# An LSTM and a GRU in one loop: the GRU's candidate and new state move one tick behind its gates

## The chip, the core and the metric

The kernel runs on one core of one Trainium2 chip. The metric is the device time of one execution in microseconds (us). TensorE does the matmuls, VectorE (DVE) and ScalarE (ACT) the element-wise work, GpSimd (POOL) a few sums, SyncE (SP) issues most of the DMA transfers. Each engine takes its own instructions in the order in which they are written; semaphores order the engines among each other.

## The reference: what is computed

`x` is 32 x 128 x 512 (batch, time, features), `cond_1024` is 32 x 512. First an LSTM runs over the 128 steps, with the condition as its first state, and its output is added to `x`. Then a GRU runs over the result, with a product of the condition in each gate, and its output is added as well.

```
# LSTM step, h0 = cond, c0 = 0
a = x_t @ Wx + b + h @ Wh                   # 32 x 2048
i, f, o = sigmoid(first three quarters of a); g = tanh(last quarter)
c = f * c + i * g ;  h = o * tanh(c)
y = x + hs                                   # input of the GRU
# GRU step, g0 = 0, vz = cond @ C_z + b_z, vr and vh likewise
z = sigmoid(y_t @ W_z + g @ U_z + vz)
r = sigmoid(y_t @ W_r + g @ U_r + vr)
hh = tanh(y_t @ W + (r * g) @ U + vh)
g = (1 - z) * g + z * hh
out = y + gs
```

Both recurrences are serial. The GRU's step s needs the LSTM's step s, and inside a step of the GRU the candidate `hh` needs the gate `r`: two products in a row (`U_z, U_r`, then `U`) with element-wise work between them.

## The kernel before

A tick is one turn of the main loop. In tick t the kernel works on step t of the LSTM and on step s = t - 1 of the GRU (`LAG = 1`), so there are 129 ticks. Each engine has a function `tick(t, n, i)` with its share of the tick, and the order of its instructions is the order of the code. Nothing else sets the order: there is no scheduler.

A step has five products on TensorE, each of 48 matmuls with float16 halves (a state and a weight are split in a high and a low part, and three of the four products of the parts are taken):

- `ps_l<-wh,h2T`: the LSTM's state times Wh, 512 columns per matmul;
- `ps_g<-w,y2T`: the GRU's input times W_z, W_r and W, 384 columns;
- `ps_g<-u,g2T`: the GRU's state times U_z and U_r, 256 columns;
- `ps_l<-wx,x2T`: x of the next step times Wx, 512 columns; it depends on no recurrence;
- `ps_g<-u,rg2T`: r * g times U, 128 columns.

Before the change TensorE does them in just this order in each tick. Between them the other engines work: `gates` (sum with the bias, VectorE L541), sigmoid and tanh (ScalarE), `ig_fc`, `tg_cell` (the cell, L696 and L698), `tanh_c`, `h_nat`, its transpose `hT` (L670), its high part (ScalarE L462) and low part (VectorE L538). For the GRU: the sum of the gates `zr` (L541), its sigmoid (ScalarE L457), `rg`, `rgT`, `rg2T` high and low; then the sum of `cand`, its tanh (L479), `zc`, `g_nat`, `gT` (L763), and `g2T` high (ScalarE L485) and low. GpSimd adds `yT = xT + hT` and the output, and scales y. Four steps make a group. One tick in four turns the next group's x and works out its scales (`turn`, `lstm_scales`), one stores a finished group (`turn_out`), one makes the low part of x, one takes its largest value.

The head of the kernel is different. Weights arrive as float32, and their split needs a scale from the sum of their squares. So the first ticks carry the preparation besides the steps: ScalarE squares each weight (`wh_squared`, `w_squared`, `u_squared`, L343) and writes the high halves (`wh_high`, `w_high`, `u_high`, L346); TensorE sums the squares over the partitions (L826); VectorE works out the scales (`weight_scale`) and writes the low halves (`wh_low`, `w_low`, `u_low`, L538, half a weight slab each). As long as a weight isn't split, its products run on the float32 weights (L789, until the LSTM's step 4 and the GRU's step 8). Wh must be split before tick 4, W and U before the GRU's step 8. The preparation is spread over the ticks by hooks: `after_state`, `after_keep` and `after_cand` on VectorE, `after_state` and `after_cand` on ScalarE. In tick 1 TensorE also does the condition's three products (`ps_c<-u,h0T` and `ps_c<-o_area,h0T`), which wait for the weights C_z, C_r and C to arrive.

Of the kernel before, what the change touches and what calls it, by code (L numbers as in the profile page):

```python
# [5 lines left out]
def lstm_then_gru(nc, x, cond, wx, wh, b0, w_z, u_z, c_z, b_z, w_r, u_r, c_r, b_r, w_h, u_h, c_h, b_h, out):  # L6
# [4 lines left out]
    ALU = mybir.AluOpType  # L11
# [9 lines left out]
    LAG = 1  # L21
    FL, F = 4, 8
# [27 lines left out]
    with ExitStack() as ctx:  # L50
# [230 lines left out]
        def _(pool):  # L281
# [50 lines left out]
            add_out(T - 1, (T - 1) % U, NG - 1)  # L332

        @block.scalar
        def _(act):
# [106 lines left out]

            def tick(t, n, i):
                s, q, r = t - LAG, n % Q, n // Q
                group = 2 * i + r
                if runs_lstm(t):
                    act.wait_ge(tg_sum, t + 1)
                    nc.scalar.activation(tg_cell[:, 0:P], gates[:, 3 * P:4 * P], ACT.Tanh)  # L448
                    act.wait_ge(ifo_sum, t + 1)
                    nc.scalar.activation(ifo, ifo, ACT.Sigmoid).then_inc(ifo_done, 1)  # L450
                    act.wait_ge(cell_done, t + 2)
                    nc.scalar.activation(tanh_c[:], cell, ACT.Tanh).then_inc(tanh_c_done, 1)
                if t == T_WH:
                    after_state(t)
                if runs_gru(t):
                    act.wait_ge(zr_sum, s + 1)
                    nc.scalar.activation(zr[:], zr[:], ACT.Sigmoid).then_inc(zr_done, 1)  # L457
# [11 lines left out]
                if (q == 1 and 0 < group < NG - 1) or t == 2:  # L469
                    act.wait_ge(xT_done, group + 2)  # L470
                    act.wait_ge(scl_done, group + 2)
                    if t >= 2 * Q:
                        act.wait_ge(gates_ps, t - 1)
                    nc.scalar.mul(x2T[:, 1 - r, HI, :], xT[:, 1 - r, :], a_x(1 - r)).then_inc(x_hi, 1)
                if t != T_WH:
                    after_state(t)
                if runs_gru(t):
                    act.wait_ge(cand_sum, s + 1)
                    nc.scalar.activation(cand[:], cand[:], ACT.Tanh).then_inc(cand_done, 1)  # L479
                    if F - 1 <= s < T - 1:  # L480
                        m_next = (n - LAG + 1) % U
                        act.wait_ge(gT_done, s + 1)
                        if m_next % Q == 0:
                            act.wait_ge(scg_done, (s + 1) // Q + 1)
                        nc.scalar.mul(g2T[:, HI, :], gT[:, s % 2, :], a_g(m_next // Q)).then_inc(g_hi, 1)  # L485
# [5 lines left out]
        def _(dve):  # L491
# [112 lines left out]
            def after_state(t):  # L604
# [5 lines left out]
                if t == T_WH:  # L610
# [5 lines left out]

                    dve.wait_ge(bias1_in, 16 * GG * J)
                    dve.wait_ge(cond_ps, 1)
                    link(nc.vector.tensor_tensor(term1[:], ps_c[:, 0:GG * P], term1[:], ALU.add))

            def after_keep(t):
                if t == T_WH + 1:
                    wh_low(1, 0)
                if t == T_WH + 2:
                    wh_low(2, 1)
                if t == T_WU_SCALE:
                    weight_scale(2, 2 * K, GG, "a_w", w1_scale)
                if t == T_WU_SCALE + 1:
                    w_low(0, 0)
                if t == T_WU_SCALE + 2:  # L630
                    w_low(1, 1)
                if t == T_WU_SCALE + 3:
                    u_low(0, 0)
                if t == T_WU_SCALE + 4:
                    u_low(1, 1)

            def after_cand(t):
                if t == T_WH:

                    wh_low(0, 0)  # L640
                    wh_low(0, 1)
# [35 lines left out]
            def tick(t, n, i):  # L677
                s, q, r = t - LAG, n % Q, n // Q
                group = 2 * i + r
                m = (n - LAG) % U  # L680
                r_s = m // Q
                r_h = (n + 1) % U // Q
                r_n = (m + 1) % U // Q
                lstm, gru = runs_lstm(t), runs_gru(t)
                if lstm:
                    if q == 0:
# [4 lines left out]
                           ).then_inc(ifo_sum, 1)  # L691
                after_sums(t)
# [6 lines left out]
                if t == T_WH:  # L699

                    new_state(t, n)
                    after_state(t)
                if gru:
                    if m % Q == 0:
                        dve.wait_ge(scg_done, (group if m // Q == r else group - 1) + 1)
                    dve.wait_ge(zr_ps, s + 1)
                    undone(zr[:], ps_g[s % 2][:, 0:2 * P], r_g(r_s), term1[:, 0:2 * P]).then_inc(zr_sum, 1)
                if lstm and t != T_WH:
                    new_state(t, n)
                if gru:  # L710
                    dve.wait_ge(zr_done, s + 1)
# [261 lines left out]
```

## Time and profile before

| | us |
|---|---|
| median of 3 runs | 1243.46 |
| lowest and highest | 1242.91, 1243.78 |
| the profiled execution | 1244.18 |
| its span, first to last instruction | 1242.4 |
| TensorE busy | 1205.5 (97% of the span) |
| VectorE busy | 872.4 (70%) |
| ScalarE busy | 445.0 (36%) |
| GpSimd busy | 278.0 (22%) |

The table gives busy times of one profiled execution over its span. The time runs 1.8 us longer than the span of the same execution. Shares are averages over a head (the first 150 us, with the loading and the splitting of the weights), some 1,070 us of equal ticks, and a tail of some 20 us in which the LSTM has ended; in the head VectorE and ScalarE have more to do than in the rest.

### The profile page before, as it was taken

What the parts mean: (1) busy time and instruction counts of PE and PEld (TensorE: products, weight loads), DVE (VectorE), ACT (ScalarE), POOL (GpSimd) and SP (SyncE); (2) the same over time, 40 slices, a digit from 0 to 9 for tenths busy, and PEclk for the clock granted to TensorE, in tenths of its full rate; (3) what the DMA queues carried; (4) which work ended last, traced back from release to release, by engine and by line L of the source; (5) the groups of instructions that cost most, each with busy time, mean ns of one, the idle gap of its engine ahead of it and who ended that gap; (6) DMA issues with size and microseconds to landing.
All of it is one profiled execution on the core that took longest, in us unless ns stands there. A gap on an engine that the chain in (4) does not pass through costs nothing.

```text
span 1242.4 us, 67987 instructions
## 1 busy us (share of the span) xinstructions
PE 1205.5 (97%) x31013; PEld 763.8 (61%) x31013; DVE 872.4 (70%) x2681; ACT 445.0 (36%) x1078; POOL 278.0 (22%) x520
## 2 busy tenths in 40 slices
PE   5889999999999999999999999999999999999996
PEld 1457666666666666666666666666666666666664
DVE  2568877777777777777776777777777777677765
ACT  5555233333333333333333333333333333333332
POOL 3100222222212222222222221222222222222221
PEclk9899999999999999999999999999999999999998
DMA  9900100111110111110011111011111001110001
GB/s 304 317 9 12 20 10 14 21 20 20 21 19 6 20 21 21 20 21 12 12 21 21 20 21 20 5 19 20 21 21 21 13 11 21 20 20 12 12 8 24
DMA packets 142000, 39.50 MB, mean 32 GB/s; under 512 B 135760, under 2 KB 136016, under 8 KB 140688
## 3 DMA queue, kind: packets, MB, share of 16 engines
q1 hardware_dynamic: 140016, 34.49, 12.9%
q8 instruction: 243, 3.98, 1.3%
q0 software_dynamic: 640, 0.53, 0.2%
q14 instruction: 45, 0.37, 0.1%
q10 hardware_dynamic: 1056, 0.13, 0.1%
HBM read 26.74 MB, written 8.39 MB: 28 GB/s over the span
## 4 chain that ended last, share of the span: by engine, by line
PE 93%; SPq 3%; DVE 2%; DMA 1%; issue 1%; ACT 0%; POOLq 0%; POOL 0%; DVEq 0%
PE ps_l L780 51%; PE ps_g L780 38%; PE ps_g L789 3%; SPq L239 2%; DMA o_area<-in_L_cond_C_dram 1%; PE ps_l L789 1%; SPq L243 1%; PE ps_bound L822 0%; DVE wh L538 0%; DVE u L538 0%; DVE zr L541 0%; SPq L248 0%; SPq L250 0%; PE ps_c L789 0%; ACT zr L457 0%
## 5 line engine op out<-in xcount | busy, mean ns | idle before, releaser
L780 PE MATMUL ps_l<-wh,h2T 128*32 128x512 f16 x5952 | 344.4, 380 | 3.3 <-DVE wh L538 3.3
L780 PE MATMUL ps_l<-wx,x2T 128*32 128x512 f16 x5952 | 342.8, 379 | 0.0
L780 PE MATMUL ps_g<-w,y2T 128*32 128x384 f16 x5760 | 256.2, 327 | 0.0
L780 PEld LDWEIGHTS ps_l<-wx,x2T 128*32 128x32 f16 x5952 | 160.6, 97 | 134.2
L780 PEld LDWEIGHTS ps_l<-wh,h2T 128*32 128x32 f16 x5952 | 154.6, 97 | 138.7 <-DVE wh L538 3.6
L780 PEld LDWEIGHTS ps_g<-w,y2T 128*32 128x32 f16 x5760 | 155.3, 97 | 92.3
L320 POOL TENSOR_TENSOR yT<-xT,hT 128x128 f32<-128x128 f32 x128 | 61.9, 484 | 589.8 <-DVE hT L670 589.8
L780 PE MATMUL ps_g<-u,g2T 128*32 128x256 f16 x5760 | 178.5, 273 | 0.8 <-ACT g2T L485 0.8
L780 PEld LDWEIGHTS ps_g<-u,g2T 128*32 128x32 f16 x5760 | 154.7, 97 | 16.9 <-issue 1.2
L541 DVE SCALAR_TENSOR_TENSOR zr<-ps_g,sc,term 128x256 f32<-128x256 f32 x128 | 61.9, 484 | 108.0 <-PE ps_g L780 100.5
L304 POOL TENSOR_TENSOR o_area<-yT,gT 128x128 f32<-128x128 f32 x128 | 58.6, 458 | 307.3 <-DVE gT L763 307.3
L541 DVE SCALAR_TENSOR_TENSOR gates<-ps_l,sc,term 128x128 f32<-128x128 f32 (+1 forms) x256 | 111.4, 476 | 13.7 <-PE ps_l L789 6.3
L696 DVE TENSOR_TENSOR ig_fc<-gates,tg_cell 128x256 f32<-128x256 f32 x128 | 54.4, 425 | 76.5 <-ACT gates L450 76.4
L780 PE MATMUL ps_g<-u,rg2T 128*32 128x128 f16 x5760 | 101.9, 220 | 4.4 <-DVE rg2T L535 4.4
L780 PEld LDWEIGHTS ps_g<-u,rg2T 128*32 128x32 f16 x5760 | 90.2, 97 | 25.2 <-DVE rg2T L535 4.6
L457 ACT ACTIVATE zr<-zr 128x256 f32<-128x256 f32 x128 | 53.3, 416 | 134.8 <-DVE zr L541 134.7
L479 ACT ACTIVATE cand<-cand 128x128 f32<-128x128 f32 x128 | 39.6, 309 | 155.3 <-DVE cand L541 155.3
L485 ACT ACTIVATE g2T<-gT,sc 128x128 f16<-128x128 f32 x120 | 48.3, 402 | 125.9 <-DVE gT L763 125.9
L538 DVE SCALAR_TENSOR_TENSOR g2T<-gT,sc,g2T 128x128 f16<-128x128 f32 x120 | 42.1, 351 | 58.5 <-ACT g2T L485 58.5
L328 POOL TENSOR_TENSOR y2T<-y_scaled,y2T 128x128 f16<-128x128 f32 x120 | 68.7, 573 | 49.6 <-ACT y2T L468 49.6
L325 POOL TENSOR_SCALAR y_scaled<-yT,sc 128x128 f32<-128x128 f32 x120 | 77.1, 643 | 11.8
L448 ACT ACTIVATE tg_cell<-gates 128x128 f32<-128x128 f32 x128 | 39.6, 310 | 107.0 <-DVE gates L541 107.0
(101 smaller groups left out, 1107.3 us busy)
## 6 DMA issues: line engine op xcount, KB each, us to landing
out_dram<-o_area SPq DMA_DIRECT2D x128, 64.0 KB, 2.1
x_nat<-in_x_dram SPq DMA_DIRECT2D x126, 64.0 KB, 2.7
wh<-in_L_cond_Wx_dram SPq DMA_DIRECT2D x4, 1024.0 KB, 12.0
w<-in_L_cond_Wh_dram SPq DMA_DIRECT2D x3, 1024.0 KB, 20.4
u<-in_L_cond_Wh_dram SPq DMA_DIRECT2D x1, 1024.0 KB, 26.5
stage<-in_L_cond_W_z_dram SPq DMA_DIRECT2D x1, 1024.0 KB, 8.5
stage<-in_L_cond_W_r_dram SPq DMA_DIRECT2D x1, 1024.0 KB, 8.1
stage<-in_L_cond_W_dram SPq DMA_DIRECT2D x1, 1024.0 KB, 10.3
```

The costliest lines, as they stand in the source:

```text
L304: nc.gpsimd.tensor_tensor(oT[:, r, q, :], yT[:, q, :], gT[:, m % 2, :], ALU.add).then_inc(oT_done, 1)
L320: nc.gpsimd.tensor_tensor(yT[:, q, :], xT[:, r, P * q:P * q + P], hT[:, n % 2, :], ALU.add).then_inc(yT_done, 1)
L325: nc.gpsimd.tensor_scalar(y_scaled[:, n % 2, :], yT[:, q, :], a_y(r), None, ALU.mult).then_inc(y_scaled_done, 1)
L328: nc.gpsimd.tensor_tensor(y2T[:, q, LO, :], y_scaled[:, n % 2, :], y2T[:, q, HI, :], ALU.subtract).then_inc(y_lo, 1)
L448: nc.scalar.activation(tg_cell[:, 0:P], gates[:, 3 * P:4 * P], ACT.Tanh)
L457: nc.scalar.activation(zr[:], zr[:], ACT.Sigmoid).then_inc(zr_done, 1)
L485: nc.scalar.mul(g2T[:, HI, :], gT[:, s % 2, :], a_g(m_next // Q)).then_inc(g_hi, 1)
L538: return nc.vector.scalar_tensor_tensor(lo, value, scale, hi, ALU.mult, ALU.subtract)
L541: return nc.vector.scalar_tensor_tensor(to, ps, scale, term, ALU.mult, ALU.add)
L696: nc.vector.tensor_tensor(ig_fc[:], gates[:, 0:2 * P], tg_cell[:], ALU.mult).then_inc(ig_fc_done, 1)
L780: mm = nc.tensor.matmul(bank[B * j:B * j + B, c0:c1].rearrange("p (n c) -> p n c", c=B), still(a, k), moving(b, k, j), start=opens and (a, ...
L789: mm = nc.tensor.matmul(bank[rows(j), c0:c0 + weights.shape[1] // J].rearrange("p (n c) -> p n c", c=B), still[:, B * chunk:B * chunk + B] ...
```

## The change

`LAG` stays 1 and `LAG2 = 2` is added: the loop has 130 ticks. In tick t the kernel now does step t of the LSTM, the gates of the GRU's step t - 1, and the candidate and the new state of the GRU's step t - 2. `runs_gru` is split in `runs_gates` and `runs_cand`. The same instructions run as before, on the same data, in another order on every engine:

- TensorE: the candidate's product of step t - 2 comes straight behind the LSTM's product; the product of g with U_z, U_r comes last in the tick, behind the one with Wx. The condition's products move from tick 1 to tick 2, behind the LSTM's third step.
- VectorE: the sum of `cand` stands behind the sum of `gates`; `zc`, `g_nat`, `gT` behind the cell; `zr`, `rg`, `rgT`, `rg2T`, `keep` at the tick's end.
- ScalarE: the tanh of `cand` stands behind the LSTM's sigmoid, the high part of `g2T` behind `tanh_c`, the sigmoid of `zr` behind the high parts of h and y.
- Preparation: `after_keep` and VectorE's `after_cand` are gone; what they did stands in `after_state`, in one piece per tick. ScalarE's `after_state` and `after_cand` now follow each other directly behind the sigmoid of `zr`.

```diff
+    LAG2 = 2
@@ ticks
-            for t in range(T + LAG):
+            for t in range(T + LAG2):
@@ ScalarE
+                if runs_cand(t):
+                    act.wait_ge(cand_sum, t - LAG2 + 1)
+                    nc.scalar.activation(cand[:], cand[:], ACT.Tanh).then_inc(cand_done, 1)
+                if runs_lstm(t):
                     act.wait_ge(cell_done, t + 2)
                     nc.scalar.activation(tanh_c[:], cell, ACT.Tanh).then_inc(tanh_c_done, 1)
...
+                if runs_gates(t):
+                    act.wait_ge(zr_sum, s + 1)
+                    nc.scalar.activation(zr[:], zr[:], ACT.Sigmoid).then_inc(zr_done, 1)
+                if q == 1 and 0 < group < NG - 1:
+                    x_high(t, r, group)
                 if t != T_WH:
                     after_state(t)
-                if runs_gru(t):
-                    act.wait_ge(cand_sum, s + 1)
-                    nc.scalar.activation(cand[:], cand[:], ACT.Tanh).then_inc(cand_done, 1)
...
                 after_cand(t)
@@ VectorE, after_state
+                    wh_low(0, 0)
+                    wh_low(0, 1)
+                    wh_low(1, 0)
                     dve.wait_ge(bias1_in, 16 * GG * J)
                     dve.wait_ge(cond_ps, 1)
                     link(nc.vector.tensor_tensor(term1[:], ps_c[:, 0:GG * P], term1[:], ALU.add))
-            def after_keep(t):
-                if t == T_WH + 1:
-                    wh_low(1, 0)
-                if t == T_WH + 2:
-                    wh_low(2, 1)
...
-            def after_cand(t):
...
                 if t == T_WH + 1:
                     wh_low(1, 1)
                     wh_low(2, 0)
+                    wh_low(2, 1)
                 if t == T_WH + 2:
                     wh_low(3, 0)
                     wh_low(3, 1)
                 if t == T_WU_SCALE:
+                    weight_scale(2, 2 * K, GG, "a_w", w1_scale)
                     weight_scale(3, 2 * K + GG, GG, "a_u", u1_scale)
                     common(2, 1)
                 if t == T_WU_SCALE + 1:
+                    w_low(0, 0)
                     w_low(0, 1)
                     w_low(1, 0)
...
@@ TensorE
+                if t == LAG2:
+                    pe.wait_ge(wh_scale, 1)
+                    for g in range(GG):
+                        pe.wait_ge(c1_in[g], 16)
+                        done = gate_as_given(ps_c, g, h0T, c_raw[g], range(K), True, True)
+                    done.then_inc(cond_ps, 1)
+                s2 = t - LAG2
+                if s2 > 0 and s2 < F:
+                    pe.wait_ge(rgT_done, s2)
...
+                    gate_as_given(ps_g[s2 % 2], 2, rgT, u_raw[2], range(K), False, True).then_inc(cand_ps, 1)
+                elif s2 > 0:
...
+                    pe.wait_ge(rg_hi, s2 - F + 1)
+                    product(ps_g[s2 % 2], 2 * P, 3 * P, u_of(2, 3), state_of(rg2T), 0, WAIT, False, False)
...
-                if t == 1:
-                    pe.wait_ge(wh_scale, 1)
...
-                    done.then_inc(cond_ps, 1)
```

TensorE in ticks 1 to 4, before (a name behind the arrow with `h0T` is the condition's product, with `gT` the gates', with `rgT` the candidate's; `stage,yT` is the GRU's input):

```order
L789 MATMUL ps_g<-stage,yT 32x128 x48
L789 MATMUL ps_c<-u,h0T 32x128 x32
L789 MATMUL ps_c<-o_area,h0T 32x128 x16
L789 MATMUL ps_l<-w,hT 32x512 x12
L789 MATMUL ps_l<-u,hT 32x512 x4
L789 MATMUL ps_g<-stage,yT 32x128 x48
L789 MATMUL ps_g<-stage,gT 32x128 x32
L789 MATMUL ps_g<-stage,rgT 32x128 x16
L789 MATMUL ps_l<-w,hT 32x512 x12
L789 MATMUL ps_l<-u,hT 32x512 x4
```

The same place after the change (from the end of tick 1 to the end of the LSTM's product in tick 3, then the candidate's):

```order
L778 MATMUL ps_g<-stage,yT 32x128 x48
L778 MATMUL ps_l<-w,hT 32x512 x12
L778 MATMUL ps_l<-u,hT 32x512 x4
L778 MATMUL ps_c<-u,h0T 32x128 x32
L778 MATMUL ps_c<-o_area,h0T 32x128 x16
L778 MATMUL ps_g<-stage,yT 32x128 x48
L778 MATMUL ps_g<-stage,gT 32x128 x32
L778 MATMUL ps_l<-w,hT 32x512 x12
L778 MATMUL ps_l<-u,hT 32x512 x4
L778 MATMUL ps_g<-stage,rgT 32x128 x16
```

The condition's products went behind the LSTM's third product, and the candidate's product behind the LSTM's fourth.

ScalarE from the middle of tick 2 to the middle of tick 4, before (`o_area,sums<-stage` squares a weight, `tg_cell<-gates` opens a tick):

```order
L343 ACTIVATE o_area,sums<-stage 128x2048
L479 ACTIVATE cand<-cand 128x128
L343 ACTIVATE o_area,sums<-stage 128x2048 x2
L448 ACTIVATE tg_cell<-gates 128x128
L450 ACTIVATE gates<-gates 128x384
L452 ACTIVATE tanh_c<-tg_cell 128x128
L457 ACTIVATE zr<-zr 128x256
L462 ACTIVATE h2T<-hT,sc 128x128
L343 ACTIVATE o_area,sums<-stage 128x2048
L479 ACTIVATE cand<-cand 128x128
L343 ACTIVATE o_area,sums<-stage 128x2048 x2
L448 ACTIVATE tg_cell<-gates 128x128
```

The same place after the change:

```order
L489 ACTIVATE zr<-zr 128x256
L345 ACTIVATE o_area,sums<-stage 128x2048 x3
L457 ACTIVATE tg_cell<-gates 128x128
L459 ACTIVATE gates<-gates 128x384
L462 ACTIVATE cand<-cand 128x128
L465 ACTIVATE tanh_c<-tg_cell 128x128
L476 ACTIVATE h2T<-hT,sc 128x128
L489 ACTIVATE zr<-zr 128x256
L345 ACTIVATE o_area,sums<-stage 128x2048 x3
L457 ACTIVATE tg_cell<-gates 128x128
```

The three squares of a tick now stand in one piece between the sigmoid of `zr` and the next tick's first tanh.

VectorE in ticks 2 and 3, from the new state of the LSTM on, before (`wh<-w,cols,wh` is a low half of Wh):

```order
L666 TENSOR_TENSOR h_nat<-gates,tanh_c 128x128
L670 STREAM_TRANSPOSE hT<-h_nat 128x128
L714 TENSOR_TENSOR rg<-zr,g_nat 128x128
L716 STREAM_TRANSPOSE rgT<-rg 128x128
L730 SCALAR_TENSOR_TENSOR keep<-zr,g_nat 128x128
L538 SCALAR_TENSOR_TENSOR wh<-w,cols,wh 128x1024
L538 SCALAR_TENSOR_TENSOR x2T<-xT,sc,x2T 128x512
L541 SCALAR_TENSOR_TENSOR cand<-ps_g,sc,term 128x128
L538 SCALAR_TENSOR_TENSOR wh<-w,cols,wh 128x1024 x2
L756 TENSOR_TENSOR zc<-zr,cand 128x128
```

The same place after the change:

```order
L662 TENSOR_TENSOR h_nat<-gates,tanh_c 128x128
L666 STREAM_TRANSPOSE hT<-h_nat 128x128
L546 SCALAR_TENSOR_TENSOR wh<-w,cols,wh 128x1024 x3
L546 SCALAR_TENSOR_TENSOR x2T<-xT,sc,x2T 128x512
L549 SCALAR_TENSOR_TENSOR zr<-ps_g,sc,term 128x256
L747 TENSOR_TENSOR rg<-zr,g_nat 128x128
L749 STREAM_TRANSPOSE rgT<-rg 128x128
L755 SCALAR_TENSOR_TENSOR keep<-zr,g_nat 128x128
```

Three low halves now stand ahead of the sum of `zr`; before, `zr`, `rg` and `rgT` came ahead of them.

## Rows read from the trace of the kernel before

**Rows 1.** Who TensorE waited for: microseconds in total, times, longest.
```profile
PE ps_g L780 <- DVE rg2T L535: 4.4, 3, 2.0
```

**Rows 2.** Busy time in a stretch: its length, each engine's, clock, DMA share, GB/s.
```profile
160.00:1160.00 1000.00, 1000.00 (x26235) 634.69 (x26227) 718.46 (x2262) 341.12 (x900) 233.23 (x436) 1.00 0.11 18
```

**Rows 3.** Timeline of one steady tick, TensorE: start, length, then the operation.
```profile
1199.23 0.84 PE L780 MATMUL ps_g<-u,rg2T 128*32 128x128 f16 x48
...
1199.90 2.76 PE L780 MATMUL ps_l<-wh,h2T 128*32 128x512 f16 x48
...
1202.49 2.12 PE L780 MATMUL ps_g<-w,y2T 128*32 128x384 f16 x48
...
1204.44 1.48 PE L780 MATMUL ps_g<-u,g2T 128*32 128x256 f16 x48
...
1205.75 2.76 PE L780 MATMUL ps_l<-wx,x2T 128*32 128x512 f16 x48
...
1208.34 0.84 PE L780 MATMUL ps_g<-u,rg2T 128*32 128x128 f16 x48
```

**Rows 4.** Timeline of steady ticks, VectorE.
```profile
1196.87 0.48 DVE L541 SCALAR_TENSOR_TENSOR zr<-ps_g,sc,term 128x256 f32<-128x256 f32 x1 [0.98 <-PE ps_g L780]
...
1198.51 0.29 DVE L535 TENSOR_SCALAR rg2T<-rgT,sc 128x128 f16<-128x128 f32 x1
...
1200.86 0.29 DVE L756 TENSOR_TENSOR zc<-zr,cand 128x128 f32<-128x128 f32 x1 [0.38 <-ACT cand L479]
...
1201.51 0.31 DVE L763 STREAM_TRANSPOSE gT<-g_nat 128x128 f32<-128x128 f32 x1
...
1202.72 0.87 DVE L541 SCALAR_TENSOR_TENSOR gates<-ps_l,sc,term 128x128 f32<-128x128 f32 x2
```

**Rows 5.** Timeline of the head, TensorE.
```profile
51.96 1.93 PE L789 MATMUL ps_c<-o_area,h0T 128*32 128x128 f32 x32 [1.46 <-DMA o_area<-in_L_cond_C_dram]
...
64.95 1.08 PE L789 MATMUL ps_g<-stage,rgT 128*32 128x128 f32 x32 [1.74 <-DVE rgT L716]
...
80.59 4.46 PE L780 MATMUL ps_l<-wh,h2T 128*32 128x512 f16 x48 [3.29 <-DVE wh L538]
...
84.98 0.39 PE L826 MATMUL ps_c<-sums,ones 128*128 128x6 f32 x2
...
145.99 2.78 PE L780 MATMUL ps_l<-wh,h2T 128*32 128x512 f16 x48
```

**Rows 6.** Timeline of the head, ScalarE and VectorE.
```profile
55.13 0.42 ACT L457 ACTIVATE zr<-zr 128x256 f32<-128x256 f32 x1 [4.06 <-DVE zr L541]
...
60.17 0.29 ACT L448 ACTIVATE tg_cell<-gates 128x128 f32<-128x128 f32 x1
...
78.06 2.47 DVE L538 SCALAR_TENSOR_TENSOR wh<-u,cols,wh 128x1024 f16<-128x1024 f32 x2
...
78.40 1.89 ACT L343 ACTIVATE o_area<-stage 128x2048 f16<-128x2048 f32 x1
...
80.47 1.91 ACT L343 ACTIVATE o_area<-stage 128x2048 f16<-128x2048 f32 x1
...
92.06 0.15 DVE L519 TENSOR_REDUCE powers<-ps_c 128x1 f32<-128x3 f32 x1
...
93.18 0.71 DVE L566 STREAM_TRANSPOSE xT<-x_nat 128x512 f32<-128x512 f32 x1
...
95.20 3.88 ACT L346 ACTIVATE w<-stage,cols 128x2048 f16<-128x2048 f32 x2
...
98.99 0.29 ACT L448 ACTIVATE tg_cell<-gates 128x128 f32<-128x128 f32 x1
...
99.72 0.42 DVE L696 TENSOR_TENSOR ig_fc<-gates,tg_cell 128x256 f32<-128x256 f32 x1 [1.30 <-ACT gates L450]
```

**Rows 7.** Timeline of the tail, TensorE.
```profile
1226.17 0.85 PE L780 MATMUL ps_g<-u,rg2T 128*32 128x128 f16 x48 [2.03 <-DVE rg2T L535]
...
1226.98 3.48 PE L780 MATMUL ps_g<-w,y2T 128*32 128x384 f16 x48
```

More of the change, by code:

```diff
@@ L691, in tick @@
                            ).then_inc(ifo_sum, 1)
+                if runs_cand(t):
+                    if s2 > 0:
+                        dve.wait_ge(cand_ps, s2)
+                    undone(cand[:], ps_g[s2 % 2][:, 2 * P:3 * P], r_g(m2 // Q), term1[:, 2 * P:3 * P]).then_inc(cand_sum, 1)
                 after_sums(t)
@@ L698, in tick @@
                     nc.vector.tensor_tensor(cell, ig_fc[:, 0:P], ig_fc[:, P:2 * P], ALU.add).then_inc(cell_done, 1)
[L699 to L721 removed]
+                if runs_cand(t):
+                    dve.wait_ge(cand_done, s2 + 1)
+                    nc.vector.tensor_tensor(zc[:], zr[:, 0:P], cand[:], ALU.mult).then_inc(zc_done, 1)
+                    dve.wait_ge(zc_done, s2 + 1)
+                    dve.wait_ge(keep_done, s2 + 1)
+                    nc.vector.tensor_tensor(g_nat[:], zc[:], keep[:], ALU.subtract).then_inc(g_done, 1)
+                    dve.wait_ge(g_done, s2 + 2)
+                    if s2 >= 2:
+                        dve.wait_ge(oT_done, s2 - 1)
+                    nc.vector.transpose(gT[:, s2 % 2, :], g_nat[:]).then_inc(gT_done, 1)
+                if lstm:
+                    new_state(t, n)
+                if F - 1 <= s2 < T - 1:
+                    if (m2 + 1) % Q == 0:
+                        dve.wait_ge(scg_done, (s2 + 1) // Q + 1)
+                    dve.wait_ge(g_hi, s2 + 2 - F)
+                    lo_part(g2T[:, LO, :], gT[:, s2 % 2, :], a_g((m2 + 1) % U // Q), g2T[:, HI, :]).then_inc(g_lo, 1)
                 if FL - 1 <= t < T - 1:
@@ L898, in tick @@
                     product(ps_g[m % 2], 0, GG * P, w_of, y_of(m % Q), HALF, END, False, False)
-                if t == 1:
-                    pe.wait_ge(wh_scale, 1)
-                    for g in range(GG):
-                        pe.wait_ge(c1_in[g], 16)
-                        done = gate_as_given(ps_c, g, h0T, c_raw[g], range(K), True, True)
-                    done.then_inc(cond_ps, 1)
-                recurs = gru and s > 0
+                if FL - 1 <= t < T - 1:
+                    if t == FL - 1:
+                        pe.wait_ge(wx_split, K)
+                    pe.wait_ge(ifo_sum, t + 2 - NL)
+                    if q == Q - 1:
+                        pe.wait_ge(x_lo, group + 1)
+                    product(ps_l[(t + 1) % NL], 0, GL * P, wx_of, x_of((n + 1) % U // Q, (n + 1) % Q), 0, END, True, False)
+                if q == 0 and 0 < group < NG - 1:
+                    bound(1 - r, group + 1)
+                recurs = 0 < s < T
                 if recurs and s < F:
```

154 lines of the change are left out of this document (56 added, 98 removed).

## The prediction, written before the changed kernel was run

> **What bounds the kernel now.** I first read where TensorE waits. In the table of waits its largest item between two equal ticks is the one for `rg2T`, 4.4 us in 3 times, so nearly none of the 128 ticks has it [rows 1]. The table of stretches says the same of the middle: in 1000 us TensorE is busy for 1000 us, at a granted clock of 1.00, VectorE for 718 and ScalarE for 341 [rows 2]. A steady tick lasts from the candidate's product at 1199.23 to the next at 1208.34, so 9.11 us, and the reader should see that the starts split it in 0.67, 2.59, 1.95, 1.31 and 2.59 us for matmuls of 128, 512, 384, 256 and 512 columns [rows 3]. That is 5.1 to 5.2 ns for each column of a product, in proportion to the work. Nothing is left over for a fixed wait.
>
> The Trainium skill (Trainium Kernel Development and Optimization, Best Practices) warns that the busy share of matmuls is no measure of the distance to the limit. By that rule alone the 1000 of 1000 could hide bubbles that a new order might close, and 0.1 us closed in each tick would be 12 us. The proportion of the starts to the columns [rows 3] speaks against it here, so I count no gain in the middle.
>
> What is left is the head, up to the product `ps_l<-wh,h2T` at 145.99 with which tick 10 begins, and the tail behind the LSTM's last product. In the head TensorE stands still for single stretches: 1.46 us for the weight C, 1.74 for `rgT`, 3.29 for the low halves of Wh [rows 5].
>
> **The steady ticks after the change.** The work is the same, only rotated: wh (2.59), candidate (0.67), w (1.95), wx (2.59), gates (1.31). Each recurrence must fit under what lies between its two products.
> - Gates to candidate. The sum of `zr` starts 0.23 us behind the product, the high part of `rg2T` 1.64 later and ends 0.29 later [rows 4]: 2.16. The cover was wx, 2.59, and is now wh, 2.59. In one tick in four the group's largest value stands between the sum of `zr` and `rg`; about 0.6 us, but `rg` waits about as long for the sigmoid anyway. Slack 0.4, as before.
> - Candidate to gates. Cover 1.95 + 2.59 = 4.54, before 2.59 + 1.95. VectorE now does it behind the LSTM's cell. The sum of `gates` starts 0.23 behind the LSTM's product (2.49 to 2.72 in [rows 3, 4]) and lasts 0.87, the sum of `cand` follows, then the waits for ScalarE, `ig_fc`, cell, `zc`, `g_nat`, `gT`; with the durations 0.42, 0.29 and 0.31 [rows 4, 6] `gT` ends some 3.4 us and the high part of `g2T` some 3.9 behind the LSTM's product, where 0.67 + 4.54 = 5.2 are there. It fits.
> - The LSTM keeps 0.67 + 1.95 + 2.59 + 1.31 = 6.5; the new state ends some 4.0 behind, its low part 4.9. It fits, also with the 1.6 us of `turn` and the scales in one tick in four.
> So the 119 steady ticks change by 0. If a tick lost the 0.4 us of slack and 0.1 more, it would cost 12 us over all, and I keep this as a rival. They can't gain, see above.
>
> **The head.** Here VectorE and ScalarE set the time, and I replay both in the order that they now have. Prices: a square 2.07 (78.40 to 80.47), a high half-pair of a weight 1.89 (two take from 95.20 to 98.99), two low halves 2.39 to 2.47, so 1.2 for one, a small operation of the scales 0.15 with gaps of 0.04, a turn 0.71 [rows 6]. From the tick's first tanh (`tg_cell`) to `ig_fc` 0.73, then `ig_fc` 0.42, four sums of 0.29 and two transposes of 0.31 with small gaps, 2.3: the new state `hT` ends 3.04 behind the tanh, and `gT` 2.46 behind it, because it stands ahead of `hT` now [rows 4, 6].
>
> The condition's product first. TensorE begins the LSTM's third step at 46.1 instead of behind the condition, ends it at 49.6, and then waits for C, which lands at 51.96 [rows 5]; the condition ends at about 53. That gains nothing: VectorE goes in order, and ahead of the gates of tick 2 stand three low halves of Wh, the sum with the condition and `zr`, whose sigmoid ends 0.15 later than the 55.55 of before [rows 6]. ScalarE then writes two high parts and starts tick 2 at 59.5, where it was 60.17 [rows 6].
>
> Then the new order bites. Before, the squares of a tick were cut by the candidate's tanh, and the low halves on VectorE ran beside them. Now ScalarE's piece waits for the sum of `zr`, this sum stands behind all low halves of its tick, and these stand behind the new state, which needs the first tanh, behind ScalarE's piece of the tick before. The two pieces follow each other instead of running side by side:
> - tick 2: tanh 59.5, `hT` 62.55, three low halves 3.6 and x's low part 0.7, sum of `zr` at 66.8; the squares begin 0.83 later.
> - tick 3: three squares, tanh at 73.75; `hT` 76.8, h's parts 0.75, two low halves 2.4: Wh is split at 80.0, so the LSTM's product starts at 80.05 (before 80.59), but the candidate of step 2 is still owed. Sum of `zr` at 79.95, squares of U from 80.78.
> - tick 4: squares end at 86.95. TensorE's sum of squares, at 84.98 before [rows 5], waits for them until 87.0 and holds the queue. Then candidate, w, wx, the bound and gates, as float32 0.87 + 2.62 + 2.59 + 0.24 + 1.75: 95.4. VectorE does the scales (two times six, four, a turn, five) until 96.1.
> - tick 5: two high parts, tanh 100.7, `hT` 103.8, three low halves; sum of `zr` at 108.1 where TensorE offers it at 106.1. The candidate's product waits 1.3 us.
> - tick 6: x's and three high parts, 6.3 us, tanh 115.25; gates wait 1.95 us for `gT`. Low halves, x's low part: sum of `zr` 123.55, the candidate waits 3.1 us.
> - ticks 7 and 8: low halves of U. Only a wait of 0.8 us in tick 9 is left. Tick 10's LSTM product starts at 153.8.
> Against 145.99 this is 7.8 us late with full clock.
>
> The clock: after a wait of 3.29 us the LSTM's product lasted 4.46 instead of 2.76 to 2.78, +1.7; after 1.74 us of waiting the next one ran with 1.08 for 32 matmuls, at full speed; in the tail, after 2.03 us, w lasted 3.48 instead of 2.12 [rows 3, 5, 7]. So a wait between 2 and 3.3 us costs about 1.5 us more. Such waits are now ahead of the candidate's products in ticks 4 (2.5 to 4.4 us) and 7 (3.1), and the one of 6.5 us for the first `gT` in tick 2, whose loss is counted above. VectorE is late too in tick 4, so I take 0.6 there and the full 1.7 in tick 7. Head: 7.8 + 2.3 = 10.1, between 7.8 (no loss) and 10.8 (both in full).
>
> The Trainium skill (TensorE: Matmul & The Clock Gate, What's actually happening) holds the halved clock for the default, released by sustained activity. By that each of the waits of ticks 5, 6 and 9 would be paid at 1.2 GHz too, some 2 us more; the row with 1.74 us speaks against it.
>
> **The tail.** Ahead of the LSTM's last product the candidate of step 125 is owed, 0.67. Before, behind that product came w, gates of step 126, a wait of 2.03 for `rg2T`, candidate, w (at half clock), gates, 2.03 again, candidate, and the output [rows 1, 7]. Now candidate, w, then the gates wait for `g2T`: 6.45 behind the product's start against 5.2, so 1.3. Then the same sequence. Owed 0.67 and 1.3, less 0.1 by a shorter wait: +1.8. The extra tick brings no work of its own, and the output's transfers stay.
>
> **The sum.** 10.1 + 1.8 = 11.9 over the profiled execution's 1244.18 (span 1242.4 and 1.8 around it), which lies 0.7 above the median; on the median 1255.4.
>
> **Rivals.**
> 1. The pieces overlap more than I replay, and only the tail and the owed products cost: +1.8 to +5, so 1245 to 1248.5. For it: fourteen links were chained by hand, and a tenth off in each is more than 1 us. Against it: the instructions' order is fixed, and 6 or 7 us of squares in one piece can't be hidden under a tick's first half.
> 2. The steady ticks lose their cover. 0.1 us in each of 119 is 12 us, 0.3 in one of four 9: 1264 to 1268 with the head. For it: slack 0.4, and the sum of `cand` now stands ahead of `ig_fc`. Against it: the same slack held in every tick before [rows 1].
> 3. Faster. The third step of the LSTM begins 7.6 us earlier. If ScalarE reached the first tanh of tick 3 by about 71.6, Wh would be split 2 us sooner than in my replay, the 3.29 us of waiting and its 1.7 of slow clock would shrink or go, up to -5, against 1.8 in the tail: 1240. It decides at that tanh; my replay has it at 73.75, with three squares (6.2) between sum of `zr` and it. The point is 2.1 us away.
>
> **Numbers.** Forecast 0.72, rival 1 0.10, rival 2 0.10, rival 3 and other gains 0.08. The likeliest has its own range of 1251 to 1259. To hold 8 of 10 the range reaches a good part of rival 1 and stops short of most of rival 2: 1247 to 1262. About 0.2% (2.5 us) is what a measurement of this kernel tells from no change: slower by more 0.88, within 0.06 (the lower part of rival 1 and the smallest gains), faster 0.06.
>
> **What would show it.** In the profile of the changed kernel: the tick's period stays 9.11 and the middle 1000 of 1000; ScalarE's tanh of tick 3 near 73.8; TensorE's sum of squares near 87 with a wait for ScalarE ahead of it; waits of 1 to 3 us for `rgT` and `gT` in ticks 5 to 7; tick 10's product near 156 (153.8 + 2.3); and one more wait in the tail, for `g2T`. I'm wrong if the product of tick 10 starts before 149, or if the period is not 9.11.

## The result, and the profile after

The changed kernel takes 1255.68 us (median of 4 runs, 1254.8 to 1257.16) against 1243.62 (4 runs, 1242.91 to 1245.37) for the kernel before. The ratio is 1.0101, with a 95% interval of 1.0086 to 1.0117: slower by 12.1 us. The forecast was 1255.4 with a range of 1247 to 1262.

The profiled execution of the changed kernel has a span of 1255.3 us, 12.9 more than before. First the waits of TensorE (engine, tile, line, releaser: us in total, times, longest):

```profile
PE ps_g L778 <- DVE gT L707: 8.1, 3, 5.3
...
PE ps_c L815 <- ACT o_area L345: 4.2, 1, 4.2
PE ps_g L778 <- DVE rgT L749: 4.1, 3, 2.8
PE ps_g L769 <- DVE rg2T L543: 4.1, 2, 2.0
...
PE ps_l L769 <- DVE wh L546: 1.8, 1, 1.8
...
PE ps_g L769 <- ACT g2T L471: 1.0, 1, 1.0
```

Against [rows 1] `rg2T` went from three waits to the two of the tail. New are 8.1 us for `gT` in the head, 4.2 for ScalarE's squares (`o_area`), and 1.0 for `g2T` in the tail. The wait for `rgT` in the head was 1.74 [rows 5] and is 4.1, the one for the low halves of Wh was 3.29 and is 1.8. The middle of the run (length of the stretch, busy time and instructions of TensorE, its weight loads, VectorE, ScalarE, GpSimd, then the granted clock, the DMA share and GB/s):

```profile
160.00:1160.00 1000.00, 1000.00 (x26247) 634.70 (x26243) 721.65 (x2266) 328.61 (x900) 239.53 (x436) 1.00 0.11 18
```

This is [rows 2] again, 1000 of 1000, with 12 matmuls more on record. A steady tick has the new order and the old length, 9.11 us from 1204.96 to 1214.07 as in [rows 3] (timeline: start, length, operation):

```profile
1204.96 0.84 PE L769 MATMUL ps_g<-u,rg2T 128*32 128x128 f16 x48
1205.63 2.12 PE L769 MATMUL ps_g<-w,y2T 128*32 128x384 f16 x48
1207.58 2.76 PE L769 MATMUL ps_l<-wx,x2T 128*32 128x512 f16 x48
1210.17 1.48 PE L769 MATMUL ps_g<-u,g2T 128*32 128x256 f16 x48
1211.48 2.76 PE L769 MATMUL ps_l<-wh,h2T 128*32 128x512 f16 x48
1214.07 0.84 PE L769 MATMUL ps_g<-u,rg2T 128*32 128x128 f16 x48
```

So the loss is in the head and the tail. The head, TensorE's timeline with its waits in brackets:

```profile
43.15 0.39 PE L815 MATMUL ps_c<-sums,ones 128*128 128x4 f32 x2
...
62.49 3.38 PE L778 MATMUL ps_g<-stage,gT 128*32 128x128 f32 x64 [5.26 <-DVE gT L707]
...
80.43 2.77 PE L769 MATMUL ps_l<-wh,h2T 128*32 128x512 f16 x48 [1.84 <-DVE wh L546]
87.44 0.56 PE L815 MATMUL ps_c<-sums,ones 128*128 128x6 f32 x2 [4.24 <-ACT o_area L345]
87.94 1.93 PE L778 MATMUL ps_g<-stage,rgT 128*32 128x128 f32 x32
89.65 4.33 PE L778 MATMUL ps_g<-stage,yT 128*32 128x128 f32 x96
...
112.12 1.08 PE L778 MATMUL ps_g<-stage,rgT 128*32 128x128 f32 x32 [0.55 <-DVE rgT L749]
...
120.01 1.95 PE L778 MATMUL ps_g<-stage,gT 128*32 128x128 f32 x64 [1.60 <-DVE gT L707]
...
127.37 1.93 PE L778 MATMUL ps_g<-stage,rgT 128*32 128x128 f32 x32 [2.81 <-DVE rgT L749]
129.07 3.41 PE L778 MATMUL ps_g<-stage,yT 128*32 128x128 f32 x96
...
157.57 2.77 PE L769 MATMUL ps_l<-wh,h2T 128*32 128x512 f16 x48
```

The last row is tick 10, at 145.99 in [rows 5]: 11.6 us later. Of these, 0.9 are not the change's. The first row, the sum of Wh's squares, is at 43.15, in the kernel before at 42.24, and up to there both do the same and wait for the same transfers. The difference is one product of x with Wx, which starts at 34.20 and 34.19 and lasts 5.58 and 4.69 us. In the profiles of all the kernels below, this point lies between 41.9 and 43.3, so I count the head from it to tick 10: 114.4 us, in the kernel before 103.8. That leaves 10.7.

What TensorE waits for is made by ScalarE and VectorE (timelines of both, `...` where rows are left out):

```profile
67.30 0.47 DVE L549 SCALAR_TENSOR_TENSOR zr<-ps_g,sc,term 128x256 f32<-128x256 f32 x1
67.81 0.42 ACT L489 ACTIVATE zr<-zr 128x256 f32<-128x256 f32 x1 [5.29 <-DVE zr L549]
68.13 1.89 ACT L345 ACTIVATE o_area<-stage 128x2048 f16<-128x2048 f32 x1
...
74.21 0.29 ACT L457 ACTIVATE tg_cell<-gates 128x128 f32<-128x128 f32 x1
...
74.95 0.42 DVE L695 TENSOR_TENSOR ig_fc<-gates,tg_cell 128x256 f32<-128x256 f32 x1 [4.34 <-ACT gates L459]
...
77.90 2.48 DVE L546 SCALAR_TENSOR_TENSOR wh<-u,cols,wh 128x1024 f16<-128x1024 f32 x2
80.29 0.48 DVE L549 SCALAR_TENSOR_TENSOR zr<-ps_g,sc,term 128x256 f32<-128x256 f32 x1
...
80.80 0.42 ACT L489 ACTIVATE zr<-zr 128x256 f32<-128x256 f32 x1 [3.27 <-DVE zr L549]
81.13 1.90 ACT L345 ACTIVATE o_area<-stage 128x2048 f16<-128x2048 f32 x1
...
87.21 0.29 ACT L457 ACTIVATE tg_cell<-gates 128x128 f32<-128x128 f32 x1
```

These rows show an alternation. ScalarE idles 5.29 us for VectorE's sum of `zr`, then squares for 6 us. VectorE idles 4.34 us for ScalarE, whose tanh comes at 74.21 behind the squares. Then VectorE's low halves end just ahead of the next sum of `zr`, for which ScalarE has idled again, 3.27 us. Each engine waits for the other in turn.

The tail of the changed kernel:

```profile
1229.70 2.76 PE L769 MATMUL ps_l<-wh,h2T 128*32 128x512 f16 x48
1232.29 0.84 PE L769 MATMUL ps_g<-u,rg2T 128*32 128x128 f16 x48
1232.96 2.12 PE L769 MATMUL ps_g<-w,y2T 128*32 128x384 f16 x48
1236.10 1.49 PE L769 MATMUL ps_g<-u,g2T 128*32 128x256 f16 x48 [1.01 <-ACT g2T L471]
1239.63 1.47 PE L769 MATMUL ps_g<-u,rg2T 128*32 128x128 f16 x48 [2.03 <-DVE rg2T L543]
```

The kernel before has its last product of the LSTM here:

```profile
1218.12 2.76 PE L780 MATMUL ps_l<-wh,h2T 128*32 128x512 f16 x48
```

From the LSTM's last product to the end of the span it is 1255.3 - 1229.70 = 25.6 us. The candidate of step 126 starts 9.93 us behind that product; before, it was 1226.17 [rows 7] less 1218.12, 8.05. So it is 1.9 later now. Behind it TensorE ran at its lower clock for a part of the time in both profiles, and for longer in the one of before: its last candidate lasted 1.24 us, here 0.85. So 25.6 stands against 1242.4 - 1218.12 = 24.3, +1.3. Other profiles have the tail with all products at full clock: 24.4 to 24.5 us in five of the kernels below that have the lag of two ticks, and 22.8 and 22.7 in the two with the lag of one. At an equal clock the tail costs 1.7.

### The profile page after: what moved, and what is told of

Its sections match the earlier page's. It is cut to its first block, busy times and chain, and to the rows that moved or that the text cites. A ratio compares the mean times of both kernels' runs of the same rounds, so it can differ in the third digit from the quotient of the medians.

```text
span 1255.3 us, 67983 instructions
## 1 busy us (share of the span) xinstructions
PE 1207.6 (96%) x31013; PEld 764.6 (61%) x31013; DVE 876.0 (70%) x2681; ACT 430.9 (34%) x1078; POOL 284.8 (23%) x520
## 4 chain that ended last, share of the span: by engine, by line
PE 89%; DVE 4%; ACT 3%; DMA 2%; issue 1%; SPq 0%; POOLq 0%; POOL 0%; DVEq 0%; ACTq 0%
PE ps_l L769 49%; PE ps_g L769 37%; DMA u<-in_L_cond_Wh_dram 2%; PE ps_g L778 1%; ACT o_area L345 1%; PE ps_l L778 1%; DVE wh L546 1%; DVE w L546 1%; ACT w L348 0%; DVE u L546 0%; ACT u L348 0%; ACT wh L348 0%; DVE zr L549 0%; PE ps_bound L811 0%; DVE ig_fc L695 0%
## 5 line engine op out<-in xcount | busy, mean ns | idle before, releaser
L769 PEld LDWEIGHTS ps_l<-wh,h2T 128*32 128x32 f16 x5952 | 159.9, 97 | 136.9 <-DVE wh L546 2.1
L769 PEld LDWEIGHTS ps_g<-w,y2T 128*32 128x32 f16 x5760 | 148.8, 97 | 67.0 <-issue 1.0
L769 PEld LDWEIGHTS ps_g<-u,g2T 128*32 128x32 f16 x5760 | 151.4, 97 | 24.1 <-ACT g2T L471 1.4
L769 PEld LDWEIGHTS ps_g<-u,rg2T 128*32 128x32 f16 x5760 | 93.1, 97 | 30.3 <-DVE rg2T L543 4.6
L328 POOL TENSOR_SCALAR y_scaled<-yT,sc 128x128 f32<-128x128 f32 x120 | 89.6, 747 | 11.8
L323 POOL TENSOR_TENSOR yT<-xT,hT 128x128 f32<-128x128 f32 x128 | 73.1, 571 | 39.6 <-DVE hT L666 31.8
L482 ACT CAST y2T<-y_scaled 128x128 f16<-128x128 f32 x120 | 35.8, 298 | 129.5 <-POOL y_scaled L328 129.5
L459 ACT ACTIVATE gates<-gates 128x384 f32<-128x384 f32 x128 | 66.9, 522 | 26.3 <-DVE gates L549 26.3
L747 DVE TENSOR_TENSOR rg<-zr,g_nat 128x128 f32<-128x128 f32 x127 | 36.8, 290 | 46.8 <-ACT zr L489 46.8
```

The source lines that it names most:

```text
L323: nc.gpsimd.tensor_tensor(yT[:, q, :], xT[:, r, P * q:P * q + P], hT[:, n % 2, :], ALU.add).then_inc(yT_done, 1)
L328: nc.gpsimd.tensor_scalar(y_scaled[:, n % 2, :], yT[:, q, :], a_y(r), None, ALU.mult).then_inc(y_scaled_done, 1)
L482: nc.scalar.copy(y2T[:, q, HI, :], y_scaled[:, n % 2, :]).then_inc(y_hi, 1)
L747: nc.vector.tensor_tensor(rg[:], zr[:, P:2 * P], g_nat[:], ALU.mult).then_inc(rg_done, 1)
L769: mm = nc.tensor.matmul(bank[B * j:B * j + B, c0:c1].rearrange("p (n c) -> p n c", c=B), still(a, k), moving(b, k, j), start=opens and (a, ...
```

## The experiments

Each ratio is to the kernel before, run on the same chip in turn. Where a head is given, it is counted in the profile as above, from the sum of Wh's squares to the LSTM's product of tick 10: 103.8 us in the kernel before, 114.4 in the changed one.

**VectorE's pieces cut.** The third low half of a tick goes behind `keep`, in ticks 1, 2, 5, 6, 7 and 8:

```diff
-                    wh_low(1, 0)
...
+            def after_keep(t):
+                if t == T_WH:
+                    wh_low(1, 0)
...
                                                    ).then_inc(keep_done, 1)
+                after_keep(t)
```

> The changed kernel, with the third low half of each tick moved behind `keep` on VectorE, as its last work in the tick; ScalarE's pieces stay whole. My theory (the head is a chain of ScalarE's and VectorE's pieces, one behind the other): the sum of `zr` comes 1.2 us sooner in ticks 2, 5, 6, 7 and 8, so the chain is 3 to 5 us shorter, 1251 to 1253 us against the changed kernel's 1255.7. ScalarE's squares stay in one piece, so TensorE's sum of squares still comes after 85 us. Rival (the lag of two ticks itself costs, by the order of the products and the extra tick): no change, 1255.7.

1248.5 us, ratio 1.0041 (1.0027 to 1.0054), 7.2 under the changed kernel, where I expected 3 to 5. The head is 106.8 us. TensorE's first gates' product starts at 60.23 instead of 62.49; 1.1 of that is the earlier sum of Wh's squares (42.08), the other 1.2 is one low half, because tick 1's piece became shorter too, which I had left out of the expectation. Of the waits in ticks 5 to 9 two are left (1.17 and 1.62). The sum of squares waits as long as before the cut:

```profile
70.86 0.29 ACT L457 ACTIVATE tg_cell<-gates 128x128 f32<-128x128 f32 x1
...
77.09 2.77 PE L778 MATMUL ps_l<-wh,h2T 128*32 128x512 f16 x48 [1.73 <-DVE wh L546]
84.10 0.36 PE L824 MATMUL ps_c<-sums,ones 128*128 128x6 f32 x2 [4.24 <-ACT o_area L345]
```

The first row is the first tanh of tick 3, the second the LSTM's product of tick 4. It starts 3.5 us sooner than in the kernel before [rows 5], and this kernel is still 5.1 us slower than that one.

**ScalarE's pieces cut.** Two of three squares or high parts, and all of Wh's high parts, go ahead of the sigmoid of `zr`, where ScalarE idled; the third stays behind it:

```diff
                 if t == T_W_SQUARES:
+                    w_squared(0)
                     w_squared(1)
-                    w_squared(2)
...
-                if t == T_WH:
-                    after_state(t)
                 if t == 2:
                     x_high(t, r, group)
+                after_state(t)
                 if runs_gates(t):
                     act.wait_ge(zr_sum, s + 1)
...
-                if t != T_WH:
-                    after_state(t)
                 after_cand(t)
```

> The changed kernel, with ScalarE's pieces cut: all four high parts of Wh, and two of each three squares or high parts, ahead of the sigmoid of `zr`, one behind it; VectorE as in the changed kernel. My theory: the first tanh of tick 2 comes near 57 instead of 60.1 us, that of tick 3 near 67 instead of 74.2, TensorE's sum of squares near 77 instead of 87.4, and only the waits for `rgT` in ticks 6 and 9 stay: 1238 to 1242 us, faster than before. Rival (the lag itself costs): 1255.7 or a little less. Second rival (the high parts and squares are long enough to delay the sigmoid of `zr` as much as they delayed the tanh): 1250 to 1256.

1238.87 us, ratio 0.996 (0.9948 to 0.9972): 16.8 under the changed kernel and faster than the kernel before, with the lag of two ticks in place. The profiled execution took 1236.98, 1.9 less than the median; one other was as short, the other four lie between 1238.6 and 1239.9. In the profile the head is 95.2 us, the first tanh of tick 2 came at 57.19, that of tick 3 at 67.48, the sum of squares at

```profile
77.49 0.36 PE L810 MATMUL ps_c<-sums,ones 128*128 128x6 f32 x2 [0.45 <-ACT o_area L345]
```

as expected. The second rival falls too: the sigmoid of `zr` wasn't held up much, and what TensorE waits for `rgT` from tick 3 on is 1.08, 0.26 and 0.74 us.

**Both cuts.**

> Both cuts together in the changed kernel. My theory: no wait of TensorE above 1 us between 57 and 140 us, tick 10's product near 137 instead of 157.6 us, 1.3 us of loss in the tail stays: 1234 to 1238 us, faster than the kernel before. Rival (the lag itself costs): not under 1250.

1237.49 us, ratio 0.9954 (0.9941 to 0.9966). That is 1.4 less than with ScalarE's pieces cut alone, and the two intervals overlap, so the gain of the second cut on top of the first is not shown. The three waits for `rgT` are gone; between 57 and 140 us one wait is above 1 us, where I had expected none:

```profile
60.72 3.64 PE L782 MATMUL ps_g<-stage,gT 128*32 128x128 f32 x64 [3.16 <-DVE gT L710]
...
139.15 2.77 PE L773 MATMUL ps_l<-wh,h2T 128*32 128x512 f16 x48
```

In tick 1 the low half behind `keep` stands ahead of tick 2's sum of gates, with ScalarE already free, so it delays the tanh (57.97 instead of 57.19 with ScalarE's cut alone). The wait grew from 2.54 to 3.16 us and the product behind it ran slow (3.64 instead of 1.96). Tick 10 is at 139.15 and not near 137; the head is 95.9 us.

**The condition's products back in tick 1**, nothing else:

```diff
-                if t == LAG2:
...
-                    done.then_inc(cond_ps, 1)
...
                     product(ps_g[m % 2], 0, GG * P, w_of, y_of(m % Q), HALF, END, False, False)
+                if t == 1:
+                    pe.wait_ge(wh_scale, 1)
...
+                    done.then_inc(cond_ps, 1)
```

> The changed kernel with only the condition's products back in tick 1, behind the GRU's first input product. My theory: they were not on the path either way, since ScalarE's first tanh of tick 2 waits for the high parts of Wh: 1255 to 1256.5 us, no difference within 0.8. Rival (their new place is what costs, because TensorE then stands 5.3 us in tick 2 with its clock falling): 1250 to 1253.

1255.56 us, ratio 1.0096 (1.0083 to 1.011), no difference from the changed kernel; the head is 114.3 us. TensorE waits 2.6 and 1.6 us for C_r and C and then 0.6 for the first `gT`, instead of 5.26 for `gT`; the sum of squares waits 4.24 us either way.

**Both cuts, and the condition back in tick 1.**

> Both cuts in the changed kernel, as in the run of both, and the condition's products back in tick 1. Theory A (their new place is worth nothing by itself, but with ScalarE's piece cut it lets tick 2 begin sooner): the first tanh of tick 2 near 59.6 instead of 58.0, but TensorE then has its full clock for the first gates' product, which in the run of both took 3.4 us instead of 1.75; the net is 0 to 2 us more, 1237.5 to 1239.5. Theory B (the move is what makes the run of both faster than before): 1243 or more.

1236.6 us, ratio 0.9943 (0.993 to 0.9957), from another set of runs than the 1237.49 of both cuts: theory B falls, and the part of A that makes it slower isn't seen either. The first tanh of tick 2 came at 57.58; tick 10 is at 137.20, the head is 94.8 us. Even where the pieces overlap, the condition's new place shows no gain.

**The clock kept up.** In the changed kernel, 56 and 36 matmuls that nobody reads go ahead of the long waits of ticks 4 and 7; the one of tick 2 stays as it was:

```diff
+            def keep_warm(n):
+                for _ in range(n):
+                    nc.tensor.matmul(ps_bound[:, 256:384], ones16[:], ones16[:], start=True, stop=True,
+                                     skip_group_check=True)
...
                 if t == T_WU_SCALE:
+                    keep_warm(56)
                     pe.wait_ge(w1_squares, GG)
...
+                if s2 == 5:
+                    keep_warm(36)
```

> The changed kernel, with extra matmuls whose result nobody reads (128 columns each) ahead of two waits of TensorE: 56 ahead of tick 4's sum of squares, 36 ahead of tick 7's candidate, both shorter than the wait. They keep the clock up and do nothing else. If the fallen clock costs what I predicted (0.6 and 1.7, measured excess in the trace 0.9 + 1.7 and 0.9 + 0.8), the time falls by 2 to 3 us to 1253 to 1254. Rival (VectorE and ScalarE are late anyway, the clock costs nothing): 1255.7, within 0.5.

1251.98 us, ratio 1.0073 (1.006 to 1.0087), 3.7 under the changed kernel. TensorE after the extra matmuls:

```profile
82.78 3.30 PE L815 MATMUL ps_bound<-ones 128*128 128x128 bf16 x56
87.10 0.36 PE L820 MATMUL ps_c<-sums,ones 128*128 128x6 f32 x2 [1.02 <-ACT o_area L345]
87.39 1.08 PE L778 MATMUL ps_g<-stage,rgT 128*32 128x128 f32 x32
88.29 2.80 PE L778 MATMUL ps_g<-stage,yT 128*32 128x128 f32 x96
...
153.64 2.77 PE L769 MATMUL ps_l<-wh,h2T 128*32 128x512 f16 x48
```

The same two products that lasted 1.93 and 4.33 us last 1.08 and 2.80. From 87.94 to 93.80 us the changed kernel had a granted clock of 0.59, a mixture of 1.2 and 2.4 GHz; here it is 1.00 from 87.1 to 93.7. The head is 110.87 us instead of 114.42, so in the profiles the fallen clock of ticks 4 and 7 costs 3.6 us. The medians are 3.7 apart, but each has an interval of some 1.8 us on either side, which leaves room for the predicted 2.3: that the fallen clock is on the path they show, its size they don't.

**Both cuts, gates of tick 2 sooner.** Two low halves of Wh stand ahead of the condition's sum in tick 1 and none behind `keep`, three are in tick 2 (one of them behind `keep`), three in tick 3. The edit against the kernel with both cuts:

```diff
                     wh_low(0, 0)
                     wh_low(0, 1)
...
                 if t == T_WH + 1:
+                    wh_low(1, 0)
                     wh_low(1, 1)
-                    wh_low(2, 0)
...
                 if t == T_WH + 2:
+                    wh_low(2, 1)
                     wh_low(3, 0)
                     wh_low(3, 1)
...
             def after_keep(t):
-                if t == T_WH:
-                    wh_low(1, 0)
                 if t == T_WH + 1:
-                    wh_low(2, 1)
+                    wh_low(2, 0)
```

> Both cuts, and one low half of Wh fewer ahead of the condition's sum in tick 1 (two instead of three), tick 3 has three low halves instead of two. My theory (the path of the first ticks runs through VectorE's low halves): VectorE's sum of gates in tick 2 near 55.8, TensorE's first gates' product near 58.8 with a short wait and full clock, the LSTM's product of tick 4 near 73.5 instead of 76.1: 1234 to 1236. Rival (the late split of Wh in tick 3 takes it back): 1237.5.

1234.0 us, ratio 0.9926 (0.9913 to 0.9938), the fastest version: 9.5 under the kernel before and 21.7 under the changed one. The head is 93.8 us, 2.2 less than with both cuts; 1.4 more of the 3.5 between the two profiles lie ahead of the sum of Wh's squares (41.87 against 43.22), where the edit changes nothing. TensorE:

```profile
58.19 1.95 PE L781 MATMUL ps_g<-stage,gT 128*32 128x128 f32 x64 [2.33 <-DVE gT L709]
...
72.98 2.77 PE L772 MATMUL ps_l<-wh,h2T 128*32 128x512 f16 x48 [1.49 <-DVE wh L541]
75.82 0.36 PE L818 MATMUL ps_c<-sums,ones 128*128 128x6 f32 x2
```

**The kernel before, with the condition and Wh's high parts moved.**

```diff
@@ ScalarE
                     wh_high(0)
                     wh_high(1)
+                    wh_high(2)
+                    wh_high(3)
...
             def after_cand(t):
-                if t == T_WH:
-                    wh_high(2)
-                    wh_high(3)
@@ TensorE
+                if t == 2:
+                    pe.wait_ge(wh_scale, 1)
...
+                    done.then_inc(cond_ps, 1)
...
-                if t == 1:
...
-                    done.then_inc(cond_ps, 1)
```

> The kernel before (candidate in the same tick as its gates), with two edits: the condition's products behind the LSTM's third product, and the high parts 2 and 3 of Wh ahead of the sigmoid of `zr` in tick 1. It asks if the gain of the run of both needs the lag of two ticks. Theory A (it is a matter of the pieces' order only): gates of tick 2 near 58.5 instead of 59.3, most of the 3.29 us wait for the low halves of Wh stays, 1241 to 1243. Theory B (the lag brings nothing): 1237 to 1239, as with both cuts.

1243.51 us, ratio 0.9999 (0.999 to 1.0008): no gain of more than about 1.2 us. The wait of 3.30 us for Wh's low halves and its slow product (4.46) are as in [rows 5], and the head is 103.3 us. For these two edits theory B falls; A named what stays, and its size, 0.5 to 2.5 us less, is not seen, though the smallest gains of that range fit in the interval. The squares and high parts of W and U kept their places, so this is not the kernel before with pieces cut as well as in the fastest version.

**The kernel before, in whole pieces.** Lag and products as before, only the preparation's pieces as in the changed kernel:

```diff
@@ ScalarE
                     after_state(t)
+                after_cand(t)
                 if runs_gru(t):
                     act.wait_ge(cand_sum, s + 1)
...
-                after_cand(t)
@@ VectorE
+                after_keep(t)
+                after_cand(t)
                 if gru:
                     if m % Q == 0:
...
-                after_keep(t)
...
-                    after_cand(t)
```

> The kernel before, lag of one tick and products in their old order, but with its preparation in whole pieces as the changed kernel has them: ScalarE's work of a tick in one piece behind the sigmoid of `zr` and ahead of the candidate's tanh, VectorE's low halves and scales in one piece ahead of the sum of `zr`. Theory (whole pieces that wait for each other cost, whatever the lag): each of ticks 2, 3 and 5 to 8 loses 1 to 4 us, 1252 to 1262 us. Rival (the pieces hurt only together with the candidate's move): 1243 to 1246.

1254.52 us, ratio 1.0095 (1.0078 to 1.0112). The head is 114.3 us, against 114.4 in the changed kernel: without the lag and without the new order of the products, the whole pieces alone make the head's loss. What the changed kernel has on top is the longer tail. Its waits of TensorE:

```profile
PE ps_g L789 <- DVE rgT L718: 10.7, 6, 5.2
...
PE ps_g L789 <- DVE gT L763: 3.5, 2, 2.4
PE ps_c L826 <- ACT o_area L343: 2.4, 1, 2.4
```

## Why the prediction was right, point by point

- **The steady ticks change by 0**: right. Period 9.11, the middle 1000 of 1000. The product that covers the wait for `rg2T` there is another one now, of the same 2.59 us. Rival 2 fell.
- **The head is a chain of ScalarE's and VectorE's pieces**: right. With the 0.9 us of the start taken off, the tanh of tick 3 came at 73.3 (predicted 73.75), the sum of squares at 86.5 (87.0), waits of 0.55, 1.60 and 2.81 us behind them (1.3, 1.95, 3.1), 0.74 in tick 9 (0.8). Cutting the pieces took the loss away and more, and whole pieces gave it to the kernel before. Rival 1, pieces that overlap, fell.
- **The head with full clock, 7.8 us**: with the clock kept up in ticks 4 and 7 the head is 110.87 us against 103.75 in the kernel before, so 7.1 measured.
- **The clock, 2.3 us**: the term that was mis-sized. I took 0.6 in tick 4, since VectorE would be late there too. The trace has the candidate and w at the lower clock, wholly or in part, for 1.71 and 4.15 us from start to start instead of 0.87 and 2.62, 2.4 in sum, and VectorE then waited 1.00 us for TensorE at the sum of `zr` of tick 4: it was less late than I took it to be. In tick 7 it is 1.45 (predicted 1.7). Keeping the clock up shortened the head by 3.6. Part of the error is one execution's: from the sum of squares to the LSTM's product of tick 5 the changed kernel took 10.9 us, with VectorE's cut and with the condition back in tick 1 it was 10.1 after the same wait of 4.24 us, and with the clock kept up 8.4.
- **The head's sum**: two errors of opposite sign, 0.7 too much for the chain and 1.3 too little for the clock, made it come out at 10.7 where 10.1 was predicted. That the forecast of 1255.4 is only 0.3 us from the median is in part luck, by these two errors and because single executions of the changed kernel differ by more than 2 us. The upper bound of 10.8 was also added up wrongly: with 1.7 in full in both ticks it is 7.8 + 3.4 = 11.2.
- **The rule for the clock**: too simple. I took 1.5 us for any wait between 2 and 3.3. After 2.54 us (ScalarE's pieces cut) and 2.66 us (the kernel before in whole pieces) the next product ran at full clock. My other reading, that even the short waits of ticks 5, 6 and 9 would be paid at 1.2 GHz, fell: the products behind 0.55, 1.60 and 0.74 us of waiting lasted 1.08, 1.95 and 1.08, as at full clock.
- **The tail, 1.8 us**: right, 1.7 at an equal clock. The wait for `g2T` is there, 1.01 (predicted 1.3), and the candidate of step 126 starts 1.9 later. In the two profiles compared here the sum came out at 1.3, since more of the last products ran at the lower clock in the one of before.
- **The condition's product gains nothing**: right, tested with and without the cuts.
- **Rival 3, faster**: it made the tanh of tick 3, by 71.6, the point that decides. The changed kernel had it at 74.2. With ScalarE's pieces cut it came at 67.5, and that kernel is faster than before. But with VectorE's cut alone it came at 70.86 and the LSTM's product of tick 4 started 3.5 us sooner than in the kernel before, and the kernel was still 5.1 us slower: TensorE then waited 4.24 us for ScalarE's squares. So this point doesn't decide. An earlier split of Wh alone doesn't make the kernel faster as long as ScalarE's pieces of the next ticks stay whole.

Whether the lag of two ticks itself brings something is only partly shown. With whole pieces it brings nothing in the head (114.4 us with it, 114.3 without), and it costs 1.7 in the tail. With it and well-cut pieces the kernel is 9.5 us faster than before, in which `rg`, `rgT` and the sum of `zr` already stood ahead of the low halves. No run has the lag of one tick with pieces cut as well as that, so part or all of the 9.5 may be had without the lag.

## What to carry to other kernels

When in-order engines hand work to each other, look at what stands between two hand-overs. A piece of 4 to 6 us of preparation that nobody waits for soon still delays everything behind it. Two such pieces on two engines, each ahead of what the other needs, add up instead of overlapping. Cut the piece at the hand-over: put the short work that somebody waits for first, and the preparation in the gaps in which the engine would wait anyway. TensorE was busy for 97% of the span; of the other 37 us, 26 lay in the first 160 us and 11 in the tail. In that head the order of the two other engines moved the whole kernel by 22 us.

## What the runs showed of the hardware that was not expected

- In tick 2, in the middle of a product with no semaphore wait, TensorE stood still for 1.10 us with no releaser in the trace:

```profile
55.93 1.30 PE L778 MATMUL ps_g<-stage,yT 128*32 128x128 f32 x40 [1.10 <-issue]
```

  In all kernels with the condition's products in tick 2 and the lag of two ticks it is there (0.5 to 1.4 us), and with these products back in tick 1 it was in the condition's own product once (1.28) and not in another run. In the kernel before with these products moved to tick 2 it isn't there. Where it is in tick 2, a wait of 2.3 us or more for `gT` follows it, so it cost nothing. Its cause stays open.
- GpSimd's sum `yT`, 0.46 us in the other ticks from 1 to 6, lasted 1.40 us in tick 2, while VectorE wrote low halves of Wh; in those other ticks no low half was written beside it. Nobody waited for it. That the one slows the other is not shown.
- The clock after a wait is not a matter of the wait's length alone. After 3.16 us of waiting the product lasted 3.64 us instead of 1.95, after 2.54 us 1.96. The same wait of 2.03 us in the tail was followed, behind the short product of the candidate, by a product of w that lasted 3.48 us in the profile of the kernel before, and 2.13 in two others with the lag of one tick. The tail as a whole was 24.3 us there and 22.7 to 22.8 in those two, and with the lag of two ticks it was 25.6 us in three profiles and 24.4 to 24.5 in five. So before an edit is given credit for 1 or 2 us, the products behind the waits have to be compared for their clock.
